# A two-layer conv and attention hybrid: the head of its first layer put in another order, its values kept on chip

## The reference

```python
# x: (8, 128, 32, 32)
scale = bn_gamma * rsqrt(bn_var + 1e-5) * dw_w;  shift = bn_beta * dw_w
h = (x - bn_mean) * scale + shift                  # per channel
qkv = einsum('oc,bchw->bohw', pw_w, h)             # then 4 heads, q, k, v
attn = softmax(q . k / sqrt(32))                   # over all pixels
x = out_w @ (attn . v) + out_b + x
t = tokens(x)
t = t + attention_1(layernorm(t))                  # 64 heads of 2, causal
t = t + experts(layernorm(t))                      # 8 experts, BN + relu, gated
```

## Time and profile before

| | |
|---|---|
| median of 3 executions | 3492.77 us (3489.22 to 3493.51) |
| the profiled execution: own time, span | 3492.9 us, 3491.2 us |
| PE busy | 3107.8 us, 89% |
| ACT busy | 2715.2 us, 78% |
| DVE busy | 2051.0 us, 59% |
| POOL busy | 270.8 us, 8% |
| DMA, mean over the span | 40 GB/s |

### The profile page before, as it was taken

How to read it: one execution, slowest core, us unless ns; L and a number is a source line. 1 busy time by engine, 2 the same in 40 slices (tenths; PEclk the granted TensorE clock), 3 DMA queues, 4 the chain that set the end, 5 groups by cost and what they waited for, 6 DMA issues and landing times.

```text
span 3491.2 us, 70941 instructions
## 1 busy us (share of the span) xinstructions
PE 3107.8 (89%) x27805; PEld 1114.7 (32%) x27805; DVE 2051.0 (59%) x2956; ACT 2715.2 (78%) x2578; POOL 270.8 (8%) x365
## 2 busy tenths in 40 slices
PE   5799999999669899998999999999998988898999
PEld 2344444444212222222222222222222222233443
DVE  3688888888636546646646646646646634433333
ACT  3444444445369999999999999999999999983555
POOL 5100000000201001001001001001001000000000
PEclk9899999999879999999999999999999999999999
DMA  4521111120020210200200210210110211001000
GB/s 177 141 51 47 50 36 50 44 51 20 5 56 17 60 26 17 60 26 17 57 26 20 57 26 19 50 34 17 43 44 17 44 41 35 17 17 58 12 13 14
DMA packets 135648, 141.00 MB, mean 40 GB/s; under 512 B 29238, under 2 KB 113300, under 8 KB 135324
## 3 DMA queue, kind: packets, MB, share of 16 engines
q1 hardware_dynamic: 135324, 136.52, 15.3%
HBM read 74.51 MB, written 55.61 MB: 37 GB/s over the span
## 4 chain that ended last, share of the span: by engine, by line
ACT 36%; PE 36%; issue 19%; DVE 4%; SPq 2%; POOL 2%; DMA 1%; DVEq 0%; ACTq 0%; POOLq 0%
ACT arena L935 35%; PE ps L1269 6%; PE ps L1322 3%; PE ps L1316 3%; PE ps L1013 3%; PE ps L1060 3%; PE ps L1357 3%; PE ps L1087 3%; PE ps L1221 2%; PE ps L1062 2%; PE ps L1071 2%; PE ps L1042 2%; DVE arena L1436 1%; DVE arena L1443 1%; SPq L524 1%
## 5 line engine op out<-in xcount | busy, mean ns | idle before, releaser
L935 ACT ACTIVATE arena<-ps 128x1536 f32<-128x1536 f32 x1536 | 2071.9, 1629 | 74.4 <-PE ps L1221 73.9
L1269 PE MATMUL ps<-arena 128*32 128x512 f32 (+3 forms) x12288 | 1276.1, 511 | 1.3 <-DVE arena L1679 1.2
L1679 DVE TENSOR_TENSOR arena<-arena,causal 128x512 f32<-128x512 f32 x1024 | 664.5, 687 | 348.6 <-ACT arena L935 338.7
L1221 PE MATMUL ps<-arena 15*128 15x512 bf16 (+3 forms) x6144 | 615.4, 335 | 199.1 <-ACT arena L935 145.7
L1221 PEld LDWEIGHTS ps<-arena 15*128 15x128 bf16 x6144 | 164.2, 92 | 1139.8 <-ACT arena L935 961.4
L879 ACT ACTIVATE arena<-ps 128x512 f32<-128x512 f32 x512 | 299.7, 595 | 264.3 <-PE ps L1062 253.7
L1269 PEld LDWEIGHTS ps<-arena 128*32 128x32 f32 x12288 | 285.7, 110 | 390.7 <-issue 336.6
L1436 DVE TENSOR_REDUCE arena<-ps 128x32 bf16<-128x1024 f32 x256 | 311.1, 1215 | 119.4 <-PE ps L1042 119.4
L1443 DVE TENSOR_TENSOR arena<-arena,ps 128x512 f32<-128x512 f32 x512 | 328.8, 679 | 25.9 <-PE ps L1071 24.9
L1664 DVE COPY arena<-ps 128x512 f32<-128x512 f32 x256 | 176.5, 689 | 226.9 <-PE ps L1269 225.7
L1060 PE MATMUL ps<-arena 96*128 96x256 bf16 x1024 | 258.9, 278 | 0.3 <-ACT arena L855 0.2
(11 more groups left out here) (194 smaller groups left out, 2004.3 us busy)
## 6 DMA issues: line engine op xcount, KB each, us to landing
arena<-qstack SPq DMA_DIRECT2D x512, 30.0 KB
parts<-arena SPq DMA_DIRECT2D x8, 1536.0 KB, 5.9
arena<-parts SPq DMA_DIRECT2D x48, 256.0 KB, 5.5
arena<-parts SPq DMA_DIRECT2D x96, 128.0 KB, 2.8
arena<-kstack SPq DMA_DIRECT2D x512, 24.0 KB
qstack<-arena SPq DMA_DIRECT2D x48, 192.0 KB, 2.8
attn<-arena SPq DMA_DIRECT2D x512, 12.0 KB
arena<-arena SPq DMA_DIRECT2D x384, 16.0 KB, 1.8
```

What stands on the lines that cost most here:

```text
L935: act.activation(PR1[:, at:at + CW], bank(BPC * (f % 2), BPC), ACT.Exp).then_inc(d_exp, 1)
L1221: mm = pe.matmul(bank(at + k)[:, s * P:(s + n) * P], Ks[par][HR * h:HR * h + QROWS, j * P:(j + 1) * P], Qs[par][HR * h:HR * h + QROWS, t * ...
L1269: mm = pe.matmul(o[HR * h:HR * (h + 1), :], V1[n % 2][:, j, v:v + HR], pr[:, h * HALF + s * P:h * HALF + (s + k) * P], start=not opened[hi ...
L1679: dve.tensor_tensor(v, v, m3, ALU.min).then_inc(d_mask, 1)
```

## The change

- The sixteen parameter loads are issued by ACT instead of SP; ACT then computes one square root ahead of the weights. The experts' eight products move from the set-up to layer 1's first group of heads (experts_norms); the three small instructions on qkw move from the set-up to behind stage A.
- POOL's two affine_selects on K2 wait for the first normalization (a_bn).
- VectorE normalizes image b+1 ahead of the subtractions of image b.
- parts has three buffers, two of them in the second half of E0. A store of image b is waited for by image b+3.
- ACT copies the values to where they stay: images 0 and 1 to V0, the others to Yall. values0 in DRAM is gone; stage B loads the values of images 2 to 7 from Yall.
- SP loads the first image's queries and keys behind the store of image 1; the stores of images 2 to 7 follow.
- Before B, ACT waits for the third buffer's stores alone, and for the other two at the first exp that writes the second half of E0. TensorE waits for 38 of ACT's 40 copies.
- Loops over images are written out on SP, POOL, ACT and VectorE.

```diff
-        parts = [cut([6, T], BF16) for _ in range(2)]
+        parts = [None, None, cut([6, T], BF16)]
+        cut = Cut(NT * NH0 * QS * 4)
+        parts[0:2] = [cut([6, T], BF16) for _ in range(2)]
         rest0 = [cut([T]) for _ in range(2)]
-        v_out = [cut([T]) for _ in range(2)]
...
+            def store_parts(b):
+                sp.wait_ge(a_lo, b * 2 + 2)
+                sp.dma_start(parts0[b].rearrange("k p t -> p k t"), parts[b % 3]).then_inc(a_stored[b % 3], INC)
...
             def load_v(b, par):
-                sp.dma_start(V0[par], values0[ds(b, 1)].rearrange("o p t -> p (o t)")).then_inc(v_loaded[par], INC)
+                sp.dma_start(V0[par], Yall[:, ds(b, 1), :].rearrange("p o t -> p (o t)")).then_inc(v_loaded[par], INC)
...
+            for b in range(2):
+                store_parts(b)
+            sp.wait_ge(a_stored[0], INC)
             load_k(0, 0)
             for th in range(2):
                 load_q(0, th)
-            load_v(0, 0)
-            store_parts(B // 2 - 1)
-            for par in range(2):
-                sp.wait_ge(a_stored[par], B * INC)
+            for b in range(2, B):
+                store_parts(b)
+            for k in range(3):
+                sp.wait_ge(a_stored[k], len(range(k, B, 3)) * INC)
             load_k(1, 1)
-            load_v(1, 1)
...
+            pool.wait_ge(a_bn, 1)
             for par in range(2):
 
                 v = K2[par][3 * GK:P].rearrange("p n (y x) -> p n y x", x=GK)
...
+            for b in range(B):
+                par = b % 3
+                wait(act, a_stored[par], b // 3 * INC)
+                for k in range(2):
+                    act.wait_ge(a_mm, b * 3 + k + 1)
+                    act.activation(parts[par][:, 3 * k, :], bank(2 * k, 2), ACT.Copy).then_inc(a_hi, 1)
+                act.wait_ge(a_mm, b * 3 + 3)
+                act.activation(V0[b] if b < 2 else Yall[:, b, :], bank(4, 2), ACT.Copy).then_inc(a_hi, 1)
+                for k in range(2):
+                    act.wait_ge(a_rest, b * 2 + k + 1)
+                    act.activation(parts[par][:, 3 * k + 1, :], rest0[k], ACT.Copy).then_inc(a_hi, 1)
...
-            for par in range(2):
-                act.wait_ge(a_stored[par], B * INC)
+            act.wait_ge(a_stored[2], 2 * INC)
...
+                        if isinstance(i, int) and i == 0 and c == SUB:
+                            for p in range(2):
+                                act.wait_ge(a_stored[p], 3 * INC)
...
-            pe.wait_ge(a_hi, B * 5)
+            pe.wait_ge(a_hi, B * 5 - 2)
...
+            def normalized(b):
+                wait(dve, a_mm, b * 3 - 3)
+                dve.tensor_scalar(xbn[b % 2], X[:, b, :], cv(c_scale0), cv(c_bias0),
+                                  ALU.mult, ALU.add).then_inc(a_bn, 1)
+
+            dve.wait_ge(x_loaded_first, INC)
+            normalized(0)
+            for b in range(B):
+                if b + 1 == 2:
+                    dve.wait_ge(x_loaded_rest, INC)
+                if b + 1 < B:
+                    normalized(b + 1)
+                for k in range(2):
+                    dve.wait_ge(a_hi, b * 5 + (k + 1))
+                    wait(dve, a_lo, b * 2 + (k - 1))
+                    dve.tensor_tensor(rest0[k], bank(2 * k, 2), parts[b % 3][:, 3 * k, :],
+                                      ALU.subtract).then_inc(a_rest, 1)
```

More of the change, by code:

```diff
@@ L331, in hybrid_kernel @@
         a_bn, a_mm, a_hi, a_rest, a_lo = [sem(n) for n in ("a_bn", "a_mm", "a_hi", "a_rest", "a_lo")]
-        a_stored = [sem("a_stored_even"), sem("a_stored_odd")]
+        a_stored = [sem(f"a_stored_{k}") for k in range(3)]
         k_loaded = [sem("k_loaded_even"), sem("k_loaded_odd")]
@@ L695, in _ @@
                                             pattern=[[0, NH0], [-1, H], [0, GK]], channel_multiplier=1))
[L698 to L704, removed]
+            for b in range(B):
+                for k in range(2):
+                    pool.wait_ge(a_hi, b * 5 + 4 + k)
+                    pool.tensor_tensor(parts[b % 3][:, 3 * k + 2, :], rest0[k], parts[b % 3][:, 3 * k + 1, :],
+                                       ALU.subtract).then_inc(a_lo, 1)
             def pool_b(i):
@@ L811, in _ @@
         def _(act):
+            for k, name in enumerate(PARAMS):
+                act.dma_start(PRr[NE * k:NE * (k + 1), :], a[name]).then_inc(w_loaded, INC)
+            for k, name in enumerate(VECTORS):
+                r = NE * len(PARAMS) + k
+                act.dma_start(PRr[r:r + 1, :], a[name].rearrange("(o c) -> o c", o=1)).then_inc(w_loaded, INC)
+            act.wait_ge(eps_set, 4)
+            act.activation(eps_c[:, 4:5], eps_c[:, 2:3], ACT.Sqrt)
             act.wait_ge(w_turned, 1)
@@ L1080, in pe_b @@
                         if c % (TURN // 2) == 0:
-                            pe.wait_ge(v_loaded[par], (i + (k - L_PV) // TURN) * INC + INC)
+                            wait(pe, v_loaded[par], (i + (k - L_PV) // TURN) * INC)
                         if kb == 0:
@@ L1391, in _ @@
             chain(dve.reciprocal(cv(c_sd, 17), cv(c_sd, 17)))
[L1392 to L1396, removed]
-                chain(dve.tensor_tensor(cv(c_B, NE), cv(c_B, NE), param("L1_ffn_be" + k), ALU.add))
             chain(dve.tensor_tensor(cv(c_scale0), param("L0_conv_bn_gamma"), cv(c_sd + 2 * NE), ALU.mult))
@@ L1407, in _ @@
             chain(dve.tensor_scalar(cv(c_ck, 2), cv(c_ck, 2), 2.0 ** 0.5, None, ALU.mult))
-            def dve_a(i):
-                for par in range(2):
-                    b = i * 2 + par
-                    wait(dve, a_mm, b * 3 - 3)
-                    dve.tensor_scalar(xbn[par], X[:, ds(b, 1), :].rearrange("p o t -> p (o t)"), cv(c_scale0),
-                                      cv(c_bias0), ALU.mult, ALU.add).then_inc(a_bn, 1)
-                    for k in range(2):
-                        dve.wait_ge(a_hi, b * 5 + (k + 1))
-                        wait(dve, a_lo, b * 2 + (k - 1))
-                        dve.tensor_tensor(rest0[k], bank(2 * k, 2), parts[par][:, 3 * k, :],
-                                          ALU.subtract).then_inc(a_rest, 1)
-            dve.wait_ge(x_loaded_first, INC)
-            dve_a(0)
-            dve.wait_ge(x_loaded_rest, INC)
-            with dve.Fori(1, B // 2) as i:
-                dve_a(i)
             def dve_b(i, subs):
@@ L1656, in between, with experts_norms @@
                     dve_e(n, name, bank(6))
+            def experts_norms():
+                for c_A, c_B, k in ((c_A1, c_B1, "1"), (c_A2, c_B2, "2")):
+                    at = c_sd + NE * (k == "2")
+                    chain(dve.tensor_tensor(cv(c_A, NE), param("L1_ffn_g" + k), cv(at, NE), ALU.mult))
+                    chain(dve.tensor_tensor(cv(c_B, NE), param("L1_ffn_b" + k), param("L1_ffn_m" + k), ALU.subtract))
+                    chain(dve.tensor_tensor(cv(c_B, NE), cv(c_B, NE), cv(c_A, NE), ALU.mult))
+                    chain(dve.tensor_tensor(cv(c_B, NE), cv(c_B, NE), param("L1_ffn_be" + k), ALU.add))
             def copy_out(g, hh):
@@ L1683, in _ @@
                         copy_out(g, 0)
+                        if g == 0:
+                            experts_norms()
                         between(g, 0)
```

34 lines of the change are left out of this document (2 added, 32 removed).

## The result

The changed kernel takes **3473.12 us** (median of 7, 3463.6 to 3476.36), the kernel before in the same rounds 3492.77 (7 runs, 3489.16 to 3506.41): the medians are 19.7 us apart; the ratio of the rounds is 0.9936, 95% interval 0.9919 to 0.9952, that is 17 to 28 us less. The profiled execution of the changed kernel took 3473.84 us, its span 3472.1.

The account below looks back on a forecast made before the run. The head, set-up and stage A, was taken as serial with all after it; terms of −11.9, −4.1, −7.2, +3.9 and −0.6 summed to −19.9, from 3492.9 to 3473.0 us, range 3462 to 3482.

Parts of the forecast that it names:

- Set-up: Before stage A: weights at 9.8, products held by POOL's three selects, first projection at 18.7 instead of 30.56, −11.9 us.
- Stage A's pace: Stage A's loop: normalizing ahead gives 6.2 us an image against 7.2, including 0.8 per two-image loop for VectorE and POOL excluding each other.
- Stores and loads: Stage A: one 9 us stall at image 5, store 2 landed at 63.4, last subtraction at 82.0, −4.1 us.
- the jam: SP's queue in stage A: eighteen loads, 14.3 us, ahead of store 2, so image 5 stalls 9 us.
- No jam: Rival on stage A's queue: loads and store 2 overlap better, most of the 9 us stall goes, 3464.5; chance 0.12.
- B's start: Start of stage B: operand wait goes, −7.2 us; three small VectorE instructions wait for POOL's last two subtractions, +3.9.
- Guard: ACT's first guard copy in stage B waits only for store 5, −0.6 us.
- At nothing: Later stages: the experts' eight products, six value loads from Yall and unrolled loops were to cost nothing.
- No locks: Rival on set-up and stage B's start: small instructions slip between POOL's, projection at 16, B at once, 3466.4; chance 0.2.
- Locks and loads cost more: Rival on the head: weights at 14.6, normalizations behind POOL pairs, stall of 12, 5 us less gain, 3478; chance 0.13.
- Slower than before: Rival on stage A's loads: store 2 stands behind loads taking 27 us more, 3500; chance 0.02.
- The head is not what sets the end: Rival on stage B: its first image is held by something that does not move, gains vanish, 3490; chance 0.03.

Follow-up runs that it names:

- the spread loads: Changed kernel with the first image's eighteen loads spread behind the stores of images 1, 2, 3 and 7 instead of all behind store 1: 3456.26 us, ratio 0.99.
- the first experiment: Changed kernel with VectorE's three small instructions on qkw back in the set-up, ahead of the first normalization: 3471.05 us.
- the two edits: Three small instructions ahead of stage A, x's other six images behind the weights: 3460.26 us on the spread loads, 3469.46 on the changed kernel with loads behind store 5.

## Why the prediction was right

It said 3473.0 and the kernel took 3473.12. That is closer than its parts were, and closer than it can be told: single runs of the changed kernel took 3463.6 to 3476.36. That the number fits to 0.1 is luck; that the head is shorter by about 20, and by which waits, is the part that was reasoned.

1. *Set-up*, −11.9 foreseen, −11.8 measured; but the way there was another. The weights were to come at 9.8 and came at 12.87: what was costed as issue time saved was partly given back, because 3 MB of x now lay right behind the parameters (held back, x lets them land at 10.3). The three selects of POOL were to hold the products; with weights that late they touched one of them for 0.2. That the two errors cancel is luck of this place: POOL's selects end at 17.0 in either case, and weights at 12.87 let the products begin at 16.64. TensorE started at 10.38 in one run and at 12.87 in another, and the projections stood at 18.18 and 18.76. The Trainium skill ("DMA: Bandwidth & Descriptors", § Issuing engines are not separate DMA queues) says that DMAs of several issuing engines run on the same 16 DMA engines and interleave; it names no price. The runs agree and give one: 2 to 5 us at TensorE's start, of which the changed kernel's projection felt 0.6 (18.76 against 18.18), and that of the run whose start came at 15.39 felt 2.9 (21.09).
2. *Stage A's pace*, 6.2 us an image foreseen: the projections of images 1 to 5 start from 26.24 to 49.50, 5.8 apart. The pieces listed for the loop of two add up to 11.9 and not to 11.5; with the lock's 0.8 they would have given 6.3. The lock on the normalization is there, once in each loop of two as charged, 2.07 (at 34.31) and 2.53 (at 45.76) instead of 0.80, but the loops took 11.8 and 11.45 (projections at 26.24, 38.05, 49.50), so little or nothing of the 0.8 shows in them: this term was too large.
3. *Stores and loads*: store 2 landed at 63.2 and the gate opened at 63.26, foreseen 63.4; the wait was 10.6 instead of 9, as image 5 came sooner. Last subtraction ended at 81.34, foreseen 82.0; from the projection to it 62.6 us, which is −4.9 for −4.1. The sum took the jam as given, and the rival "No jam" doubted only how long it is; the spread loads show that it was a choice of place.
4. *B's start*: from the first scores to the reduction 4.03 us, against 0.65 before: +3.4 for +3.9, and in the first experiment it is 0.43. The wait for the operands went as foreseen, −7.1 for −7.2. The Trainium skill ("SBUF — State Buffer", § Who interferes with whom) has beside the rule on two SBUF inputs one more, that a tensor_scalar can take the shared pair too, and that a tensor_reduce never does here. The trace agrees with both: the tensor_scalar of two elements, one SBUF input, took 1.91 instead of 0.17, and in the first experiment the reduction ran beside POOL in 1.23 as always.
5. *Guard*: first to ninth reduction 16.52 us against 17.06, −0.54 for −0.6; at the seventeenth it is no longer to be seen (33.64 against 33.68).
6. *At nothing*: no later piece can be told from the scatter, which is larger than any of them (above: +8.4 in B, −8.2 in layer 1).

The first reduction was to stand at 86.5, and stood at 85.48. The terms up to there sum to −20.4 measured for −19.3 foreseen; with the guard −20.9 for −19.9. Of the rivals, "No locks" is refuted by rows (1.91 and 2.04), "No jam" and "Locks and loads cost more" by the gate at 63.26 and the weights at 12.87, "Slower than before" by the loads, which took about the 14.3 us costed (from the landing of store 1 at 45.1 to that of the last load at 59.6), and "The head is not what sets the end" by the span, 19.1 shorter for 20.4 in the head.

Three expectations failed on one cause, one of them unseen in its number. The two-buffer kernel was to cost 10 us and cost 4.1; the kernel with spread loads was to lose 4 us to the lock and lost none; the kernel with the normalization in its old place met its number since the missing lock made up for a store that came later than reasoned. I took the lock at B's start as a fixed price of the three instructions, while it depends on which engine is last in the last image. Where image 7 waits for its buffer, or its normalization comes late, VectorE is ahead of POOL and the lock does not occur.

## What to carry to other kernels

A transfer that is moved ahead of others in one queue is paid by whoever waits for those behind it: before moving eighteen loads at once, lay the queue out in time against the pace of the stage (foreseen here as 6.2 us an image, 3.7 of it a store; 5.8 measured) and give each gap as much as it holds; that was worth another 14 us in the head. A lock between two engines is a matter of phase, so moving something upstream can remove it, as in three runs here, and it should be priced by the row of the place, not by the instruction. And where one of two waits is taken away, look at what ends at the same time: holding x back started TensorE 2.5 us earlier and the projection 0.6, since POOL's selects stood right behind, and the two edits together moved B's first reduction by 0.9 us with the loads spread and by 0.4 or less with the loads behind store 5.

## What was not expected of the hardware

- A load of 0.5 KB on ACT's queue took 6.2 us to land with 3 MB on SP's queue issued 1.2 us before it; with that load held back TensorE, which waits for the same parameters, started at 10.31 to 10.43 (four runs), and in nine runs without holding between 12.43 and 15.39.
- The eighteen loads of operands moved at 220 GB/s in the changed kernel too, a row of the DMA view from 0 to 110 us in 40 slices gives it, beside stores at 400 and more:

```profile
GB/s 24 379 209 276 422 399 28 0 0 0 0 0 235 337 265 282 242 220 204 222 224 326 411 409 407 221 255 323 0 216 355 254 319 80 238 235 22 0 0 0
```

- TensorE, having stood for 10 us at the gate, ran the next image's projection at the lower of its two levels (0.5, 1.2 GHz). The view by stretches shows it (us, busy times of PE, PEld, DVE, ACT and POOL, granted clock, DMA share, GB/s), first of the changed kernel, where the stretch has 0.53, then with the loads spread, where it has 1.00 (2.4 GHz):

```profile
60.00:71.00 11.00, 5.40 (x7) 2.28 (x8) 3.54 (x4) 5.76 (x6) 3.86 (x2) 0.53 0.98 379
```

```profile
60.00:71.00 11.00, 7.48 (x43) 5.12 (x41) 5.39 (x7) 8.44 (x10) 6.65 (x3) 1.00 1.05 374
```

So a gate costs its wait and about 2.6 us more for the projection behind it (6.34 against 3.70), of which the next projection felt 2.2 (it starts 7.96 behind instead of 5.8). It does not take 10 us of standing: in the kernel before, the projection at 81.87 took 6.37 after TensorE had stood for 3.94.
